# Three more tiles' gated products transposed in blocks through DRAM, in a routed low-rank layer on one core

## The reference

```
base   = x @ W.T
logits = x @ Wr.T + 5 * onehot(the sequence's expert)
gates  = softmax over the two largest logits, 0 for the other experts
h      = x @ A[e].T            (rank 16 for each of 8 experts: 128 columns)
out    = x + base + 2 * sum over e of gates[e] * h[e] @ B[e].T
```

## Time and profile before

| | |
|---|---|
| median of three runs | 80.19 us |
| profiled execution | 80.64 us |
| its span | 78.9 us |
| TensorE matmul (PE) busy | 73.4 us, 93% |
| DVE busy | 59.0 us, 75% |
| ACT busy | 21.5 us, 27% |
| POOL busy | 22.3 us, 28% |
| granted TensorE clock | full over the whole span |
| HBM traffic | 15.5 MB, 196 GB/s over the span |

### The profile page before, as it was taken

The page is one execution under the profiler, slowest core; times in us unless marked ns, Lnnn a source line. Parts: engine busy times, 40 slices in busy tenths (PEclk is TensorE's granted clock), DMA queues, the critical chain, the costliest instruction groups (busy, mean ns, idle before and its releaser), DMA issues.

```text
span 78.9 us, 1523 instructions
## 1 busy us (share of the span) xinstructions
PE 73.4 (93%) x492; PEld 69.5 (88%) x492; DVE 59.0 (75%) x230; ACT 21.5 (27%) x56; POOL 22.3 (28%) x26
## 2 busy tenths in 40 slices
PE   6989899959999999999999999999999999999930
PEld 2259799849999999999999999999999999999920
DVE  0097487898883959797989889698979598797640
ACT  1571951405041331220405050504114131202100
POOL 4044626150641606060504223150604150000000
PEclk9999999999999999999999999999999999999999
DMA  1999993000089797186476959989933650763034
GB/s 9 314 354 362 408 427 134 0 0 8 18 204 185 259 223 240 38 224 224 69 255 130 331 102 347 382 287 368 394 157 70 205 228 0 293 239 133 8 109 157
DMA packets 11046, 15.57 MB, mean 197 GB/s; under 512 B 5920, under 2 KB 8224, under 8 KB 10912
## 3 DMA queue, kind: packets, MB, share of 16 engines
q1 hardware_dynamic: 10752, 14.96, 58.6%
q10 hardware_dynamic: 288, 0.53, 1.8%
HBM read 10.64 MB, written 4.85 MB: 196 GB/s over the span
## 4 chain that ended last, share of the span: by engine, by line
PE 78%; DMA 7%; DVE 6%; SPq 2%; ACT 1%; issue 1%; DVEq 0%
PE heads_ps L506 38%; PE base_ps L506 25%; DMA first_sb<-in_first 7%; PE base_ps L538 5%; PE heads_ps L538 5%; PE heads_ps L542 2%; PE base_ps L542 2%; DVE gate L386 2%; PE base_ps L529 1%; DVE gh L394 1%; ACT w_hi L264 1%; DVE top_at L372 1%; DVE second L381 1%; SPq L188 1%; DVE out_sb L410 1%
## 5 line engine op out<-in xcount | busy, mean ns | idle before, releaser
L237 POOL TENSOR_TENSOR x_lo<-xT_sb,x_hi 128x512 fp32r<-128x512 f32 x14 | 18.0, 1289 | 36.9 <-ACT x_hi L276 35.5
L506 PE MATMUL heads_ps<-w_hi,x_hi 128*128 128x392 f32 x63 | 21.6, 350 | 0.3 <-ACT w_hi L264 0.3
L506 PE MATMUL heads_ps<-w_lo,x_hi 128*128 128x392 f32 x63 | 20.9, 340 | 0.0
L506 PE MATMUL heads_ps<-w_hi,x_lo 128*128 128x392 f32 x63 | 20.8, 341 | 0.0
L506 PE MATMUL base_ps<-w_hi,x_hi 128*128 128x256 f32 x64 | 17.6, 285 | 0.0
L506 PE MATMUL base_ps<-w_hi,x_lo 128*128 128x256 f32 x64 | 17.6, 281 | 0.0
L506 PE MATMUL base_ps<-w_lo,x_hi 128*128 128x256 f32 x64 | 17.4, 280 | 0.0
L292 ACT ACTIVATE e<-top 128x1 f32<-128x1 f32 x16 | 4.7, 296 | 38.3 <-DVE top L369 38.3
L506 PEld LDWEIGHTS base_ps<-w_hi,x_hi 128*128 128x128 f32 x64 | 12.0, 189 | 0.5 <-ACT w_hi L264 0.5
L506 PEld LDWEIGHTS heads_ps<-w_hi,x_hi 128*128 128x128 f32 x63 | 11.6, 188 | 0.8 <-issue 0.6
L506 PEld LDWEIGHTS base_ps<-w_lo,x_hi 128*128 128x128 f32 x64 | 12.1, 189 | 0.0
(11 more groups left out here) (50 smaller groups left out, 94.7 us busy)
## 6 DMA issues: line engine op xcount, KB each, us to landing
x_sb<-in_x SPq DMA_DIRECT2D x4, 768.0 KB, 4.8
out<-out_sb SPq DMA_DIRECT2D x4, 768.0 KB, 4.0
xT_sb<-in_xT SPq DMA_DIRECT2D x5, 512.0 KB, 4.2
x_sb<-in_x SPq DMA_DIRECT2D x1, 1024.0 KB, 6.1
first_sb<-in_first SPq DMA_DIRECT2D x2, 454.0 KB, 5.9
xT_sb<-in_xT SPq DMA_DIRECT2D x1, 768.0 KB, 8.0
gh_blocks<-blocks SPq DMA_DIRECT2D x10, 64.0 KB, 2.4
ghT<-gh_blocks SPq DMA_DIRECT2D x10, 64.0 KB, 3.0
```

What stands on the lines that cost most here:

```text
L237: nc.gpsimd.tensor_tensor(x_lo[:, s, :], xT_sb[:, t - len(FIRST), :], x_hi[:, s, :].bitcast(FP32), ALU.subtract).then_inc(x_lo_made, 1)
L506: return nc.tensor.matmul(dst, xs[:, s, chunks[k]], ws[:, k, cols], start=(k == 0 and n == 0), stop=(k == KC - 1 and n == last_n))
```

## The change

`MOVED` grows from tiles 2 to 11 to tiles 1 to 13, so that TensorE transposes only tiles 0, 14 and 15. The lora products of tiles 0 and 1 go into steps 3 and 4 like all others. On SP tile 1 brings no load, tiles 12 and 13 bring neither load nor store, and three output stores stand in the loop (behind tiles 8, 9 and 10) where there were two. In the last tiles the lists of ACT, DVE and TensorE are reordered: heads 14 and 15 run whole, with lora products between them, base 14 comes before lora 13, and several additions of DVE stand behind the block transposes.

```diff
-MOVED = range(2, 12)
+STORES_FROM = 8
+MOVED = range(1, 14)
...
-        ghT_ps = {0: heads_ps[3][:, 0:P], 1: base_ps[3][:, BASE:BASE + P]}
+        ghT_ps = {0: base_ps[3][:, BASE:BASE + P]}
         for t in range(MOVED[-1] + 1, TILES):
-            ghT_ps[t] = base_ps[(t + 2) % SLOTS][:, BASE:BASE + P]
+            ghT_ps[t] = base_ps[(t + 1) % SLOTS][:, BASE:BASE + P]
...
             for t in MOVED:
                 blocks_out(t)
-                if t % 2 == 0:
+                if t % 2 == 0 and PAIRS + t - 2 < TILES:
                     sp.wait_ge(xT_group, 16 * xT_groups)
-                    load_xT(PAIRS + t - MOVED[0], 2, xT_group)
+                    load_xT(PAIRS + t - 2, 2, xT_group)
                     xT_groups += 1
-                elif x_groups <= GROUPS:
+                elif t % 2 and MOVED[0] < t and x_groups <= GROUPS:
...
                 ghT_in(t)
-                if t >= MOVED[-1] - 3 and stores < 2:
+                if t >= STORES_FROM and stores < GROUPS - 1:
                     sp.wait_ge(out_made, BATCH * stores + BATCH)
                     store(BATCH * stores, BATCH)
...
             exponential(0)
             exponential(1)
+            x_upper(3)
+            exponential(2)
             ghT_upper(0)
-            x_upper(3)
-            ghT_upper(1)
-            exponential(2)
-            for t in range(3, MOVED[-1] + 2):
+            t0, t1, t2 = range(TILES - 3, TILES)
+            for t in range(LAG, t0):
                 x_upper(t + 1)
-                if t - LAG in MOVED:
+                if t > LAG:
                     ghT_upper(t - LAG)
                 exponential(t)
...
             ghT_upper(t0 - 1)
-            ghT_upper(t0)
             exponential(t1)
             exponential(t2)
+            ghT_upper(t0)
             ghT_upper(t1)
             ghT_upper(t2)
...
             best_two(1)
-            ghT_lower(0)
             gates(1)
             gated(1)
-            out_rest(0)
-            out_base(0)
-            ghT_lower(1)
+            in_blocks(1, 1)
             best_two(2)
             gates(2)
             gated(2)
             in_blocks(2, 2)
-            out_rest(1)
-            out_base(1)
...
+            ghT_lower(t0 - 4)
+            best_two(t0 - 1)
+            out_rest(t0 - 4)
+            gates(t0 - 1)
+            gated(t0 - 1)
+            in_blocks(t0 - 1, (t0 - 1) % SLOTS)
+            out_base(t0 - 4)
             ghT_lower(t0 - 3)
             best_two(t0)
             ghT_lower(t0 - 2)
             out_rest(t0 - 3)
-            out_base(t0 - 3)
             gates(t0)
             gated(t0)
+            in_blocks(t0, t0 % SLOTS)
+            out_base(t0 - 3)
             out_rest(t0 - 2)
+            out_base(t0 - 2)
             ghT_lower(t0 - 1)
-            out_base(t0 - 2)
-            out_rest(t0 - 1)
-            out_base(t0 - 1)
-            ghT_lower(t0)
             best_two(t1)
             gates(t1)
             gated(t1)
-            out_rest(t0)
-            out_base(t0)
+            out_rest(t0 - 1)
+            out_base(t0 - 1)
             best_two(t2)
+            ghT_lower(t0)
             ghT_lower(t1)
             gates(t2)
             gated(t2)
+            out_rest(t0)
+            out_base(t0)
             out_rest(t1)
+            ghT_lower(t2)
             out_base(t1)
-            ghT_lower(t2)
             out_rest(t2)
             out_base(t2)
...
             heads_product(2, 0, 2)
-            pe.wait_ge(ident_made, 1)
-            transpose(0)
             for k in range(1, KC):
                 last = heads_product(2, k, 2)
             last.then_inc(heads_done, 1)
             base(2, (0, 1))
+            pe.wait_ge(ident_made, 1)
+            transpose(0)
+            base(2, (2, 3)).then_inc(base_done, 1)
             pe.wait_ge(b_lo_made, 1)
-            lora_of(0, 0)
-            transpose(1)
-            base(2, (2, 3)).then_inc(base_done, 1)
-            lora_of(1, 1)
-            step(3, 3, lagged=False)
-            step(4, 4, lagged=False)
+            step(3, 3 + SLOTS)
+            step(4, 4)
...
             step(t0, s0 + SLOTS)
             lora_of(t0 - 2, (t0 - 2) % SLOTS)
-            pe.wait_ge(out_made, t1 - SLOTS + 1)
-            transpose(t0 - 1)
             heads_ready(t1)
-            heads(s1, (0, 1))
-            lora_of_tail(t0 - 1)
-            heads(s1, (2,))
+            heads(s1, range(KC)).then_inc(heads_done, 1)
+            lora_of(t0 - 1, (t0 - 1) % SLOTS)
+            heads_ready(t2)
+            heads(s2, range(KC)).then_inc(heads_done, 1)
             pe.wait_ge(out_made, t2 - SLOTS + 1)
-            transpose(t0)
-            heads(s1, (3,)).then_inc(heads_done, 1)
-            heads_ready(t2)
-            heads(s2, (0, 1))
-            lora_of_tail(t0)
-            heads(s2, (2, 3)).then_inc(heads_done, 1)
-            pe.wait_ge(out_made, t0)
             transpose(t1)
             base(s1, range(KC)).then_inc(base_done, 1)
-            base_ready(t2)
+            lora_of(t0, s0)
+            pe.wait_ge(tail_lo_made, 1)
             base(s2, (0,))
             lora_of_tail(t1)
-            pe.wait_ge(out_made, t1)
+            pe.wait_ge(out_made, t2 - SLOTS + 2)
             transpose(t2)
```

More of the change, by code:

```diff
@@ L280, in ghT_upper @@
                 if t in MOVED:
-                    act.wait_ge(ghT_landed[t % 2], 16 * (t // 2 - MOVED[0] // 2 + 1))
+                    act.wait_ge(ghT_landed[t % 2], 16 * ((t - MOVED[0]) // 2 + 1))
                     nc.scalar.activation(ghT_hi[s][:, :], ghT[s][:, :], ACT.Copy).then_inc(ghT_hi_made, 1)
@@ L314, in _ @@
             exponential(1)
+            x_upper(3)
+            exponential(2)
             ghT_upper(0)
-            x_upper(3)
-            ghT_upper(1)
-            exponential(2)
-            for t in range(3, MOVED[-1] + 2):
+            t0, t1, t2 = range(TILES - 3, TILES)
+            for t in range(LAG, t0):
                 x_upper(t + 1)
-                if t - LAG in MOVED:
+                if t > LAG:
                     ghT_upper(t - LAG)
                 exponential(t)
-            t0, t1, t2 = range(TILES - 3, TILES)
             x_upper(t1)
@@ L456, in _ @@
             in_blocks(2, 2)
-            out_rest(1)
-            out_base(1)
-            for t in range(3, MOVED[-1] + 2):
-                if t - LAG in MOVED:
-                    ghT_lower(t - LAG)
+            t0, t1, t2 = range(TILES - 3, TILES)
+            for t in range(LAG, t0 - 1):
+                ghT_lower(t - LAG)
                 best_two(t)
-                if t - LAG in MOVED:
-                    out_rest(t - LAG)
-                    out_base(t - LAG)
+                out_rest(t - LAG)
+                out_base(t - LAG)
                 gates(t)
                 gated(t)
-                if t in MOVED:
-                    in_blocks(t, t % SLOTS)
-            t0, t1, t2 = range(TILES - 3, TILES)
+                in_blocks(t, t % SLOTS)
+            ghT_lower(t0 - 4)
[5 more added lines that the diff above has]
+            out_base(t0 - 4)
             ghT_lower(t0 - 3)
@@ L561, in base_ready, with step @@
                     pe.wait_ge(out_made, t - SLOTS + 1)
-            def step(t, j, lagged=True):
+            def step(t, j):
                 s = j % SLOTS
@@ L566, in step @@
                 heads(s, range(KC)).then_inc(heads_done, 1)
-                if lagged:
-                    lora_of(t - LAG, (j - LAG) % SLOTS)
+                lora_of(t - LAG, (j - LAG) % SLOTS)
                 base_ready(t)
```

## The result

The changed kernel takes 81.65 us (median of 4, 81.46 to 81.83) against 80.12 for the kernel before (4 runs, 80.03 to 80.71): ratio 1.0165, 95% interval 1.0117 to 1.0212. It is slower by 1.65%. Medians are over all executions, while ratios and intervals leave out those over 1.5% above the fastest of their kernel, so the two can differ a little. The forecast was 80.6. Its 8-in-10 range, 78.9 to 81.9, holds the time near its upper end; the forecast's own range, 80.1 to 81.2, does not. The time lies in the region of R3, which had a chance of 0.19 and whose boundary was a landing of ghT 11 later than 64.6: it landed at 64.87. The profiled execution took 81.51 with a span of 79.7.

What follows compares the result with a forecast made beforehand. TensorE was taken to bound the kernel, gapless from tile 3's heads except one 0.85 wait. Terms 0.12 - 0.22 + 1.06 - 0.54 = +0.42 gave 81.06, less 0.45 to the median: 80.6; own range 80.1 to 81.2, 8-in-10 78.9 to 81.9.

Steps and rivals of the forecast that it cites:

- R3: Slower rival at the end: ghT 11 lands later than 64.6, whole over 1% slower, 81.6 to 82.9; chance 0.19.
- The start, +0.12: Up to heads 5: removed wait 0.85 and transpose 0.11 eaten by waits of 0.5 (x_lo 3) and 0.9 (ghT_lo 0).
- R1: Rival at the start: gate 1 escapes POOL's x_lo 3, start term -0.80, time 79.7; chance 0.24.
- Who gets the shared ports: DVE against POOL: "gate" 1, 0.02 ahead of x_lo 3, taken as blocked, although the skill's first-starter rule gives -0.80.
- The middle: Middle tiles: same order on each engine, term 0, hidden behind TensorE's 4.25 us a tile.
- Transposes -0.22: End, TensorE: the transposes of tiles 12 and 13 go, 2 x 0.11.
- The moved store, +1.06: End: store of tiles 6 to 8 ahead of blocks 11 makes lora 11 late 0.38 and ghT_lo 12 late 0.68.
- stored 62.2, ghT 11 issued at 62.25 and landed at 64.25: End, SyncE: blocks 11 issued at 59.0, 3.2 us out behind the store; lora 11 starts 0.38 late.
- The second half, DVE's queue: End: work queued behind ghT_lower 11 on DVE makes ghT_lo 12 ready at 68.60, wanted 67.92: wait 0.68.
- The last store, -0.54: End, SyncE: a 1.65 us issue before the last store taken as chance; without it the store goes 0.54 earlier.
- R2: Rival at the end: the moved store does not delay blocks 11, without the +1.06, time 79.5; chance 0.12.
- The combination R1 with R2: Both rivals together, at start and end: time 78.6; chance 0.12.

Runs made afterwards that it cites:

- e2_only_front: Kernel before with only the changed start (tile 1 moved, lora 0 and 1 in steps 3 and 4), old end: 80.55 us, ratio 1.0041.
- e6_pool_waits: e1_store_back with POOL's x_lo 3 held until the gate of tile 1 is done: 79.82 us, ratio 0.9953 to before.
- e10_best: e1_store_back plus ghT_lower 0 ahead of gated 2, x_upper 3 behind the first exponential, x_lo 3 held until gate 0 is done: 78.89 us, ratio 0.9841.
- e1_store_back: Changed kernel with the third output store (tiles 6 to 8) moved out of the loop, behind ghT_in 13: 80.40 us, ratio 1.0033 to before.
- e8_dve_order: Changed kernel with ghT_lower 12 on DVE right behind the block transpose of tile 13, ahead of three additions: 81.14 us, ratio 1.0119 to before.
- e3_only_store: Kernel before with only the third output store moved into the loop, behind ghT_in 10: 82.14 us, ratio 1.0211.
- e4_before_again: Kernel before, unchanged, a single execution for a second profile: span 77.9 us, 1.0 under the first profile.
- e11_before_gate: Kernel before with x_upper 3 behind the first exponential and POOL's x_lo 3 held until gate 0 is done: 79.24 us, ratio 0.9830.
- e9_store_on_act: Changed kernel with the third store issued from ACT's queue instead of SyncE's, at nearly the same time: 81.20 us, ratio 1.0115 to before.

## Why the prediction was right and where it was off

- **The start, +0.12: right, 0.13 to 0.15.** "gate" 1 was blocked with 0.02 of lead, TensorE waited for x_lo 3 and then for ghT_lo 0, and e2_only_front shows the same +0.13 alone. The two waits were 0.64 and 0.65 by the start times where I had 0.5 and 0.9, with 0.2 in restarts that I had left out; the sum holds, the split did not. e6_pool_waits shows that the cause is the collision. R1 came true in none of the six profiles with that start.
- **Who gets the shared ports.** In nine profiles the gate of tile 1 started 0.01 to 0.04 ahead of x_lo 3, and in all nine it was blocked until POOL was done. The lock holds for a whole instruction, as the Trainium skill has it (SBUF — State Buffer, "SBUF: two separate sides"); that the first to start gets it does not hold for starts this close in the records. A lead of 0.12 in the earlier trace rows was free, and so was one of 0.3 after (18.52 against 18.82).
- **The middle: right, 0.** heads 5 to lora 11 is 38.22 in all kernels without the moved store but e10_best, where a late ghT_lo 10 costs 0.19.
- **Transposes -0.22: near.** With the store out of the way the new end is worth -0.37 (e1_store_back); the 0.15 more is in the order of the end, among it a delay of 0.10 inside lora 12 of the kernel before (0.22 from its fifth product, at 66.57, to the sixth). That split was not tried.
- **The moved store, +1.06: the mechanism right, the size too small.** The step that failed is "stored 62.2, ghT 11 issued at 62.25 and landed at 64.25". Measured: 62.86 and 64.87. In this profile the way out was 3.3 against the 3.2 I took, and the way back 2.0 as taken, but the whole began later: ghT_in 10 went at 58.59 and not at 58.09, since blocks 10 were 5.2 us on their way (4.5 before), and the schedule of TensorE was 0.12 early. So lora 11 came 1.13 late and not 0.38. The late start is not needed for the price, though. In e8_dve_order and e3_only_store blocks 10 took 4.5 and ghT_in 10 went on time (32.1 and 32.0 after heads 5, 32.1 in the kernel before), and still ghT_in 11 went 37.05 and 36.79 after heads 5, where my 62.25 is 36.25. There blocks 11 took 4.0 and 3.8 out. What was sized too small is the landing of the store, behind which the blocks came in by 0.2 or less each time, as I had assumed: I gave it the 3.5 of a store alone, and it took 3.7, 4.4 and 4.2. The second half, DVE's queue, was 0.65 for 0.68, and e8_dve_order shows that it is DVE's queue. Each wait also costs 0.11 in its restart (0.23 to the next product instead of 0.12), which I had left out. Together 1.13 + 0.65 + 0.22 = 2.0, and e1_store_back gives back 2.04. R3 was named with this boundary and this place, but mainly with a longer way back as its cause; the delay came in the way of the store and the blocks instead.
- **The last store, -0.54: wrong.** In the changed kernel it does go 0.45 after the start of out_base 15. But against e4_before_again, with 0.63, that is a gain of 0.18 and not of 0.54; to the end of the span it is some 0.35 (2.84 against 3.19). I took the long issue for chance in one execution, took its whole 0.54 off, and then took off the 0.45 between that execution and the median as well, which would hold such a chance already. And it was no chance: it came again, with 1.27. Those 0.45 were more likely its late start (0.60 against e4_before_again); no profile of the median execution shows it. Both mistakes made the forecast too fast.
- **Sum of what was measured.** The median before, the start, the order of the end, the store, and what lies behind the last product: 80.19 + 0.15 - 0.37 + 2.04 - 0.35 = 81.66, against 81.65. The agreement to 0.01 is luck, as single profiles and a span read to 0.1 stand behind it. The forecast of 80.6 missed by 1.0, about 1.0 of it in the moved store and 0.2 in the last store, less 0.15 in the order of the end; the wide range held the time.

R2 is refuted by e1_store_back and e3_only_store together. The combination R1 with R2 was built in effect as e10_best, by taking away both causes: 78.89 where 78.6 had been worked out. That these are close is in part chance, since e10_best also brings x_lo 3 forward (heads 5 at 11.10, where R1's -0.80 gives 11.46), and since 78.6 has the last store's error in it.

## What to carry to other kernels

If something waits for the landing of a small transfer, look for a large one that moves at the same time and that nobody waits for: here putting the store behind the last round trip gave back 1.1 us, and putting it on another queue did not help. Read the price to the end of the span and not only to the last product: of the 2.04 gained there 0.7 was lost again behind it. Why is not shown. When a late piece stands at the head of an in-order engine's list, price the whole list behind it and look for the next buffer that is wanted from there. Before taking an operation off the path, ask which of two engines blocks it: bringing x_lo 3 forward by 1.8 us into a free gap earned 1.7% here (e11_before_gate), while rerouting three tiles earned nothing even with the store put back (1.0033). And a stray event in one profile that the median may already leave out must not be taken off twice; a second profile of the same kernel settles it.

## What the runs showed of the hardware

- A 64 KB write to DRAM (blocks 11) beside a 768 KB store took 3.3 to 4.0 us from issue to landing in four kernels, the store being ahead of it on the same queue in three and on ACT's in one, and 1.8 to 2.6 without it in the other eight profiles. Blocks 10, with a store issued ahead and a load behind in every kernel, took 4.2 to 5.5.
- Some issues on SyncE's queue take 0.8 to 1.65 us where others take 0.3 to 0.5. The load of xT in round 10 of the loop took 1.07 to 1.27 in all twelve profiles, also where two more transfers stood ahead of it; the one in round 6 took 0.79 to 1.26 in eleven. Near 74 us one of 1.27 to 1.65 came in both profiles of the kernel before and in the four with the whole change and the store out of the loop, and none in the changed kernel, e2_only_front, e3_only_store, e8_dve_order, e9_store_on_act and e11_before_gate. Why is open; no run was made for it.
- TensorE's start after a wait costs about 0.11 us: 0.23 to the next product of 256 columns instead of 0.12. The granted clock was full there.
- DVE's cast of two columns (L374, L375) took 0.59 and 0.41 instead of 0.17 in e6_pool_waits and e8_dve_order, where it started while POOL's x_lo 2 ran, and ended within 0.03 of it.
